# Routing weights as two fp32r parts in blocks of 32 rows, one bias product per half batch, and nineteen more identity products

## The reference, cut to what matters

```python
logits = xf @ Wg + bg
probs = jax.nn.softmax(logits, axis=-1)
w, idx = jax.lax.top_k(probs, TOP_K)
w = w / jnp.sum(w, axis=-1, keepdims=True)
comb = jnp.sum(jax.nn.one_hot(idx, E, dtype=xf.dtype) * w[..., None], axis=1)
h = jax.nn.relu(jnp.einsum('nd,edh->enh', xf, W1) + b1[:, None, :])
y = jnp.einsum('enh,ehd->end', h, W2) + b2[:, None, :]
out = jnp.einsum('end,ne->nd', y, comb)
```

## Time and profile before

| | |
|---|---|
| runs before, us | 179.95, 180.94, 181.54; median 180.94 |
| profiled execution, us | 182.35 |
| its span, first to last instruction, us | 180.5 |
| PE busy in the span | 163.2 us, 712 instructions |
| DVE, ACT, POOL busy | 118.7, 102.9, 73.0 us |
| mean granted TensorE clock | 0.981 |
| DMA | 7.23 MB, mean 40 GB/s |

### The profile page before, as it was taken

One profiled execution on the slowest core, in us unless ns is written; L12 is line 12 of the kernel. 1 busy time (PEld: TensorE's weight loads), 2 busy tenths in 40 slices (PEclk: granted clock), 3 DMA queues, 4 the chain that ended last, 5 costly groups with the idle time before them and its releaser, 6 DMA issues.

```text
span 180.5 us, 2419 instructions
## 1 busy us (share of the span) xinstructions
PE 163.2 (90%) x712; PEld 96.3 (53%) x712; DVE 118.7 (66%) x380; ACT 102.9 (57%) x185; POOL 73.0 (40%) x120
## 2 busy tenths in 40 slices
PE   1999998979885799999999999999999899999992
PEld 1554655434332348555655644367667566677781
DVE  3758898984367488866568557666769664566541
ACT  3446638846753324899747577673664446645621
POOL 2399272262372043976621041352522244322500
PEclk9999999999999966999999999999999999999999
DMA  6798600000000234300000000000000000001001
GB/s 177 264 315 178 210 8 0 2 0 2 2 0 0 57 75 101 77 0 0 0 4 0 0 0 0 4 0 2 0 5 0 0 0 0 0 0 58 4 0 58
DMA packets 5570, 7.23 MB, mean 40 GB/s; under 512 B 749, under 2 KB 3606, under 8 KB 5558
## 3 DMA queue, kind: packets, MB, share of 16 engines
q1 hardware_dynamic: 5142, 6.66, 13.0%
q10 hardware_dynamic: 416, 0.42, 0.7%
HBM read 5.17 MB, written 0.52 MB: 32 GB/s over the span
## 4 chain that ended last, share of the span: by engine, by line
PE 65%; DVE 18%; ACT 8%; issue 4%; POOL 2%; DMA 1%; SPq 0%; DVEq 0%; POOLq 0%; ACTq 0%
PE bank L1120 7%; PE bank L1156 6%; PE bank L1268 5%; PE bank L1175 4%; PE bank L1270 4%; PE bank L1269 4%; PE bank L1251 3%; PE bank L1253 3%; PE bank L1252 3%; PE bank L1178 3%; DVE stats L1325 3%; PE bank L1237 3%; PE bank L914 2%; PE bank L1196 2%; POOL rstd L526 2%
## 5 line engine op out<-in xcount | busy, mean ns | idle before, releaser
L644 POOL TENSOR_TENSOR pair<-early,pair 128x512 fp32r<-128x512 f32 x16 | 20.5, 1287 | 38.6 <-ACT pair L861 38.6
L1600 DVE SCALAR_TENSOR_TENSOR pair<-bank,pair 128x512 fp32r<-128x512 f32 x32 | 21.6, 690 | 19.0 <-ACT pair L868 18.9
L1512 DVE TENSOR_REDUCE nmax<-bank 128x2 f32<-128x308 f32 x64 | 26.3, 471 | 11.4 <-PE bank L1120 11.2
L836 ACT ACTIVATE prob<-bank 128x512 f32<-128x512 f32 x40 | 22.7, 597 | 6.4 <-PE bank L1156 6.1
L1120 PE MATMUL bank<-pair,q_s 97*128 97x308 f32 x64 | 22.1, 411 | 0.7 <-ACT q_s L813 0.3
L868 ACT ACTIVATE pair<-bank 128x512 fp32r<-128x512 f32 x32 | 18.8, 596 | 6.1 <-PE bank L1253 4.8
L861 ACT ACTIVATE pair<-early 128x512 fp32r<-128x512 f32 x16 | 10.1, 632 | 21.1 <-DVE early L1596 21.1
L526 POOL TENSOR_TENSOR rstd<-vare,m_half 128x4 f32<-128x4 f32 x10 | 10.4, 1044 | 24.4 <-DVE vare L1330 21.1
L1120 PEld LDWEIGHTS bank<-pair,q_s 97*128 97x128 f32 x64 | 13.2, 214 | 12.0 <-DVE nmax L1512 7.1
L1156 PE MATMUL bank<-q_s,pair 112*128 112x512 f32 x40 | 17.5, 452 | 0.1
L1268 PE MATMUL bank<-pair,w_h 128*128 128x512 f32 x32 | 14.1, 440 | 0.0
(11 more groups left out here) (239 smaller groups left out, 314.0 us busy)
## 6 DMA issues: line engine op xcount, KB each, us to landing
w_s<-in_w SPq DMA_DIRECT2D x1, 1024.0 KB, 7.3
prob<-in_w SPq DMA_DIRECT2D x1, 1024.0 KB, 12.8
q_s<-q_late SPq DMA_DIRECT2D x12, 64.0 KB, 2.0
q_s<-pair SPq DMA_DIRECT2D x9, 64.0 KB, 2.0
x_t<-in_x SPq DMA_DIRECT2D x2, 256.0 KB, 3.1
wf_s<-in_w_ffn SPq DMA_DIRECT2D x1, 512.0 KB, 4.8
row<-in_rows SPq DMA_DIRECT2D x1, 260.0 KB, 3.9
wc_s<-in_w_ctx ACTq DMA_DIRECT2D x1, 256.0 KB, 4.1
```

The lines of the kernel that those rows point to most:

```text
L644: pool.tensor_tensor(ec_l[:, n % NEC], ec[:, n % NEC], ec_h[:, n % NEC].bitcast(F32), ALU.subtract).then_inc(ec_lo, 1)
L836: nc.scalar.activation(prob[:, u % NPR], bank[ST[u % 3]][:], ACT.Exp).then_inc(prob_ready, 1)
L1512: dve.tensor_reduce(nmax[:, b, q, j, g:g + 2], item_bank("score", n)[:, 0:2 * TK].rearrange("p (h k) -> p h k", k=TK), AX.X, ALU.max, nega ...
L1600: dve.scalar_tensor_tensor(out=hid_l[:, g % NH], in0=bank[RING[g % 4]][:], scalar=0.0, in1=hid_h[:, g % NH].bitcast(F32), op0=ALU.max, op1 ...
```

## The change: what it does

The routing weights are split into two fp32r parts instead of three bf16 ones. The parts lie in four blocks of 32 rows of which eight are used (high, low, high, low), so that the turned weights have 104 rows (3 x 32 + 8). The first two blocks feed the spreads. b2 lies in four blocks of the same kind (high, high, low, low), and one 104-row product replaces three of 24 rows. `pick_e` moves into the memory of `sel`, `comb_f` into that of `q_late`; ACT therefore waits for the last moves out of `q_late` before its first copy. b2 is loaded four times instead of three. `comb_part` is now one buffer for both batch entries, cleared once at the start by DVE, and entry 1 waits for the turn of entry 0.

The identity products grow from 35 to 54: 4, 3, 1, 1 and 2 in the first stage, one more after the second cell step, 5 ahead of `turn_in(1)` and 2 in `query(0)`.

```diff
+PART = 32
+ROWS_B2 = 3 * PART + E
...
-        b2_part = sb("b2_part", [3 * E, 3, P], BF16)
-        pick_e = sb("pick_e", [3 * E, E, P], BF16)
-        hot = sb("hot", [3 * E, E])
+        b2_h = sb("b2_h", [ROWS_B2, P], F32R)
+        b2_part = sb("b2_part", [ROWS_B2, P], F32R)
+        hot = sb("hot", [ROWS_B2, E])
...
-            for p in range(3):
-                sp.dma_start(b2_s[p * E:(p + 1) * E], b2).then_inc(ld_b2, 16)
+            for p in range(4):
+                sp.dma_start(b2_s[p * PART:p * PART + E], b2).then_inc(ld_b2, 16)
...
-                    link(pool.tensor_copy(b2_part[:, 0], b2_s[:]))
-                    link(pool.tensor_tensor(b2_r[:], b2_s[:], b2_part[:, 0], ALU.subtract))
-                    link(pool.tensor_copy(b2_part[:, 1], b2_r[:]))
-                    pool.tensor_tensor(b2_part[:, 2], b2_r[:], b2_part[:, 1], ALU.subtract).then_inc(b2_ready, 1)
+                    link(pool.memset(b2_part[:].bitcast(F32), 0.0))
+                    block_of = [slice(p * PART, p * PART + E) for p in range(4)]
+                    for rows_p, to in zip(block_of, (b2_part, b2_part, b2_h, b2_h)):
+                        link(pool.tensor_copy(to[rows_p], b2_s[rows_p]))
+                    for rows_p in block_of[2:]:
+                        pool.tensor_tensor(b2_part[rows_p], b2_s[rows_p], b2_h[rows_p].bitcast(F32), ALU.subtract)\
+                            .then_inc(b2_ready, 1)
...
+                    if b == 0:
+                        for moved in q_moved[HQ - 1:]:
+                            act.wait_ge(moved, 48)
+                    copy_out(bank[TB[0]][0:ROWS_B2], comb_f[:, b], comb_tr, b + 1,
...
+            pe.wait_ge(consts_ready, 3)
+            keep_busy(4, 7)
             key_value_bias(0)
+            keep_busy(3, 7)
...
             keys_values(0)
+            keep_busy(1, 7)
             turn_a(0)
             key_value_bias(1)
+            keep_busy(1, 7)
             queries(0)
             keys_values(1)
+            keep_busy(2, 7)
             state(0)
...
             pe.wait_ge(gates_act, 6)
-            keep_busy(7, 0)
+            keep_busy(8, 0)
...
             def turn_in(b):
+                if b == 1:
+                    keep_busy(5, 0)
...
                 b, q = divmod(m, HQ)
+                if m == 0:
+                    keep_busy(2, 0)
                 pe.wait_ge(q_lo, b + 1)
...
-                        last = pe.transpose(comb_ps[:, j * P:(j + 1) * P], comb_part[:, b, j], ident_b[:])
+                        rows_j = comb_part[:, j].bitcast(F32).rearrange("p k e -> p (k e)")[:, 0:ROWS_B2]
+                        last = pe.transpose(first[0:ROWS_B2, j * P:(j + 1) * P], rows_j, ident[:])
...
-                    for k in range(3):
-                        pe.matmul(y, b2_part[:, k], comb_f[:, b], start=k == 0, stop=False)
+                    pe.matmul(y, b2_part[:], comb_f[:, b], start=True, stop=False)
...
+                    if b:
+                        dve.wait_ge(comb_tr, b)
+                    link(dve.tensor_copy(comb_part[:, :, 0:4:2, 0:E], twice(comb[:, b])))
+                    dve.tensor_tensor(comb_part[:, :, 1:4:2, 0:E], twice(comb[:, b]),
+                                      comb_part[:, :, 0:4:2, 0:E].bitcast(F32), ALU.subtract).then_inc(comb_ready, 1)
```

More of the change, by code:

```diff
@@ L210, in two_blocks @@
         sel = sb("sel", [P, HQ, SEL_W], F32R)
+        pick_e = sel[0:ROWS_B2].rearrange("p q w -> p (q w)")[:, 0:E * P].rearrange("p (e o) -> p e o", o=P)
         k_hl = q_late[:, :, 0:NB * TKP]
@@ L241, in two_blocks @@
         comb = sb("comb", [P, NB, NJ, E])
-        comb_r = sb("comb_r", [P, NB, NJ, E])
-        comb_part = sb("comb_part", [P, NB, NJ, 3, E], BF16)
-        comb_f = k0[0:3 * E].rearrange("p c d -> p (c d)").bitcast(BF16).rearrange("p (b t) -> p b t", b=NB)
+        comb_part = sb("comb_part", [P, NJ, 4, PART], F32R)
+        comb_f = q_late[0:ROWS_B2]
         y_f = q_m
@@ L557, in _ @@
                     .then_inc(sel_ready, 1)
-            link(pool.tensor_tensor(hot[:], ident[0:3 * E, 0:E], ident[0:3 * E, E:2 * E], ALU.add))
-            pool.tensor_tensor(hot[:], hot[:], ident[0:3 * E, 2 * E:3 * E], ALU.add).then_inc(hot_ready, 1)
+            pool.tensor_tensor(hot[:], ident[0:ROWS_B2, 0:E], ident[0:ROWS_B2, PART:PART + E], ALU.add)\
+                .then_inc(hot_ready, 1)
             pool.wait_ge(hot_ready, 1)
@@ L632, in _ @@
                 if m == 4:
[L633 to L638 removed]
+                    pool.wait_ge(ld_b2, 64)
+                    link(pool.memset(b2_part[:].bitcast(F32), 0.0))
[5 more added lines that the diff above has]
+                            .then_inc(b2_ready, 1)
+                    pool.wait_ge(b2_ready, 2)
                 if m in (1, 5):
@@ L796, in pick_copies @@
                 act.wait_ge(hot_ready, 1)
-                nc.scalar.activation(pick_e[:], hot[:].rearrange("p (e o) -> p e o", o=1).broadcast_to([3 * E, E, P]),
+                nc.scalar.activation(pick_e, hot[:].rearrange("p (e o) -> p e o", o=1).broadcast_to([ROWS_B2, E, P]),
                                      ACT.Copy).then_inc(pick_ready, 1)
@@ L1236, in comb_spread @@
                     wait_item(LAST[XP[0][1]])
-                pe.matmul(bank[spread_bank(n)][:], pick_e[:, e], comb_f[:, b], start=True, stop=True)\
+                pe.matmul(bank[spread_bank(n)][:], pick_e[:, e], comb_f[0:ROWS_B2, b], start=True, stop=True)\
                   .then_inc(comb_b_mm, 1)
@@ L1258, in down @@
                 if e == 0 and c == 0:
[L1260 removed]
+                    pe.wait_ge(b2_ready, 2)
                     if b == 0:
                         pe.wait_ge(o_ev_ready, NB * HQ)
[L1263 to L1264 removed]
+                    pe.matmul(y, b2_part[:], comb_f[:, b], start=True, stop=False)
                 g = n * HC + c
@@ L1351, in _ @@
             link(dve.memset(nm_part[:], 0.0))
+            link(dve.memset(comb_part[:].bitcast(F32), 0.0))
             dve.memset(nm_part[:, :, :, :, 0:1], 1.0)
@@ L1581, in tail, with twice @@
                     link(dve.tensor_tensor(comb[:, b], hit1w[:, b], hit2w[:, b], ALU.add))
-                    link(dve.tensor_copy(comb_part[:, b, :, 0], comb[:, b]))
-                    link(dve.tensor_tensor(comb_r[:, b], comb[:, b], comb_part[:, b, :, 0], ALU.subtract))
-                    link(dve.tensor_copy(comb_part[:, b, :, 1], comb_r[:, b]))
-                    dve.tensor_tensor(comb_part[:, b, :, 2], comb_r[:, b], comb_part[:, b, :, 1],
-                                      ALU.subtract).then_inc(comb_ready, 1)
+                    def twice(ap):
+                        return ap.rearrange("p j (o e) -> p j o e", o=1).broadcast_to([P, NJ, 2, E])
+                    if b:
[3 more added lines that the diff above has]
+                                      comb_part[:, :, 0:4:2, 0:E].bitcast(F32), ALU.subtract).then_inc(comb_ready, 1)
             def scaled(n):
```

5 lines of the change are left out of this document (1 added, 4 removed).

## The result

The changed kernel takes 178.3 us (median of 6 runs, 177.59 to 179.93) against 181.24 us of the kernel before beside it (6 runs, 179.75 to 183.96). The ratio is 0.9881, 95% interval 0.9834 to 0.9929: faster by 1.2%, where 2.6% were forecast. The time lies inside the range; the case that came is the rival *Experts only*, not the likeliest.

A forecast was written before the change was run, and what follows sets the result against it. PE was taken to bound the kernel (65% of the chain of waits). Gains of 3.9 + 1.0 + 0.6 = 5.5 us took 182.35 to 176.9, and 0.7 us for the lower median gave 176.2 us; range 174.4 to 179.2.

The forecast's parts named there:

- Experts only: Rival, chance 0.26: expert gains come, the clock at 65 us still falls, first stage even or 1 us late; 177.0 to 178.5.
- Terms 1 to 3: Expert stage: spreads without gaps 2.6 us, fewer bias products 1.4, splitting and turning weights 0.2, less 0.3 for ACT/DVE: 3.9 gained.
- The gap stays: Rival, chance 0.13: switching row count or operand, not bf16, breaks the load stream; spreads gain nothing; 178.3 or 179.9 us.
- Term 3: Splitting and turning the routing weights: DVE drops two dependent operations, the f32 turn is longer; gain 0.2 us.
- The hand-over: First three spreads, in the attention: each is waited for anyway, so no gain or loss, 0 us.
- Term 5: First stage: identity products raise PE's clock sooner, partly under the DMA wait; gain 0.6 us.
- case of a rise by 9.5 us: First stage: if the clock rises by then, the added 1.9 us is about won back; gain 0.2 us.
- Term 4: Start of the second attention: eight new products in PE's idle time keep the clock up; gain 1.0 us.
- The baseline: Profiled 182.35 us against median 180.94: half of the 1.4 us difference, 0.7 us, taken off the forecast time.

The follow-up runs named there:

- routing alone: The changed kernel without its nineteen new identity products; median 176.69 us, ratio 0.9777 to before; further sets 177.59 us (0.9791) and 178.55 us (0.9884).
- the repeat of the change: The changed kernel, unaltered, run again beside two variants on the same chip; median 178.82 us, ratio 0.9861 to the kernel before.
- identity products alone: The kernel before with the nineteen new identity products and nothing else; median 181.44 us, ratio 1.0028.
- the repeat of before: The kernel before, unaltered, run again to see the granted clock of each execution; median 182.6 us, ratio 1.0005.
- extra product: The changed kernel with one more fp32r product, here of 24 rows, ahead of each of the 16 spreads; 185.66 us (one execution).

## Why the prediction was off

**Terms 1 to 3, the experts (-3.9): right in size, wrong in reason.** The stage gave 3.57 us in the profile: starts 0.23 us apart, rounds of 3.03 us, the bias from L1271 at 121.33 to L1286 at 122.27, 0.94 us, as forecast. But the 0.27 us that a spread lost was put down to the turn between fp32r and bf16; it is the price of a product of 64 rows or fewer among full ones. The forecast came out because the new spread has 104 rows, and rows 10, on which it leaned, had 97 and 112. So the size came right with the reason wrong, which is luck. The rival *The gap stays* named the row count, but gave it the wrong consequence: the change switches to a row count that costs nothing. The Trainium skill (TensorEngine Tiling (Array Packing), Overview and Tiling Modes) lists modes of 64 and of 32 rows beside the full array of 128, and says "Changing tiling mode (not just tile) drains the TensorE". The edge between 64 and 80 rows and the equal price of 24 and 64 agree with it; that it is a change of mode, or a drain, no run here shows. The prediction weighed instead what the Trainium skill says of fast loading (TensorE: Matmul & The Clock Gate, Weight-path perf modes) and gave it no weight in the sum. That was right: the load of 0.19 us hides, except at the hand-over. Term 3 had a wait of under 0.6 us before the first spread of entry 1; it is 0.67 us, where it was 0.72.

**The hand-over, costed at 0: +0.4 us.** "The first three spreads stand in the attention, each waited for anyway" holds for the wait as it was; but it is PE that waits here, and its wait grew. Timeline, PE, of the change:
```profile
112.06 0.60 PE L1242 MATMUL bank<-ident,comb_part 128*104 128x128 f32 x4
...
113.42 0.49 PE L1255 MATMUL bank<-q_late,sel 104*128 104x512 f32 x1 [0.53 <-ACT q_late L674]
```
The turn takes 0.60 us where it took 0.39, ACT's copy is waited for 0.53 us where it was 0.26, and an unhidden load of 0.19 stands where 0.09 stood. So of 3.57 us some 3.2 reach the end, and the shortest executions agree: 179.61 before, 176.46 with routing alone, 3.15 us.

**Term 5, the first stage (-0.6): this step failed.** It gave +0.51 us in the profile and +1.1 us between shortest executions (177.59 against 176.46; 180.73 against 179.61). The working had the cost about right: 1.9 us in the open if the clock does not rise sooner. Its case of a rise by 9.5 us even came, in the repeat of the change (timeline, PE):
```profile
10.69 1.10 PE L965 MATMUL bank<-a_f,w_s 128*128 128x512 f32 x2
```
ACT had the queries at 11.83 there, 0.15 us ahead of rows 3, where 0.2 were worked out. The failure was to book this as a return of the products. The upper level came by 9.5 us in some executions with no product ahead (routing alone) and at 13 or later in others; with eleven it came by 9.3 us in the repeat, by 11.4 in the first profile, and after 14 in another (identity products alone: L928 at 13.47 takes 1.06 us where 0.59 is the upper level's). One profiled execution of before, with a late rise, was taken for what every execution does. Over all profiled executions, ACT gets the first queries at 11.81 to 13.71 us in the eight with eleven products, and at 10.62 to 12.05 in the ten without the seven that stand in the open: 1.1 us later at an early rise and 1.7 at a late one. The chain of waits of the change, 3 to 14 us, shows where it lies, L1031 (start, us, what):
```profile
3.90 2.00 PE bank L932 x2
5.90 1.39 PE bank L1031 x3
7.29 0.85 PE bank L936 x2
```

**Term 4, the low clock at 65 us (-1.0): right for the profile, not for the runs.** The two profiled executions differ there by 1.25 us. But before has the low stretch in part of its executions only, and the change has it too. In the mean the late products give 0.4 us or nothing, within what the runs can tell; what they did come with is that the longest stretches are missing.

**The baseline.** The profiled execution of before (182.35 us) was longer than nearly three of four of its executions (59 of 80). Half of its distance to the median was credited as clock that could not be won back. The late products gave 0.4 us at most, so nothing in the runs supports keeping the other half.

By the shortest executions routing gives -3.2 us and the first-stage products +1.1; with -0.4 to 0 for the late ones that is -2.1 to -2.5 us. The ratio of 0.9881 is 2.1 us; the medians of all executions lie 2.9 us apart in the first set and 2.7 beside the repeat (181.49 and 178.82). By the means of all executions the same steps are -3.4, +0.9 and -0.4 us, each uncertain by about 0.4, together -2.9. So of the 5.5 us that the terms add up to, term 5 accounts for the largest miss, some 1.5 us, before term 4 and the hand-over. Routing alone has the shortest executions; its three sets have ratios of 0.9777, 0.9791 and 0.9884. In the median it does not stand clear of the versions with late products and none in the open (0.9804 to 0.9809).

## What to carry to other kernels

A product whose contraction (the rows that are summed over) has 64 rows or fewer, put singly into a stream of full ones, costs more than its length: look for starts 0.3 us apart where 0.23 is the pace, and fill the operand with zero rows to 80 or more before changing types or dropping products. Products that are only to keep the clock up belong under a wait that is there anyway, and even there their return has to be seen over many executions: the mean granted clock of each, beside its time. Where executions of one kernel lie several per cent apart, compare the shortest and the shares of long ones, and do not credit a change with a disturbance that one profiled execution happened to have.

## What the runs showed of the hardware

- Start distances at full clock are 0.23 us for 512 columns in fp32r, with 80, 104, 112 and 128 rows, and single bf16 products of 104 and 128 rows among them fit the same pace (0.69 us for three distances). Between bf16 products it is 0.22 us (the five identity products at 57.21 in the change). With 24 and 64 rows in fp32r the way in, through and out again takes 0.37 us more, with 24 rows in bf16 0.27 us more.
- Few columns of weights cost something too: the first value product, 128 rows by 32 columns, starts 0.33 us after the full one ahead of it (73.78 to 74.11, above).
- A weight load of fp32r with 104 or 128 rows takes 0.19 us and is hidden under the product before; one of 24 rows takes 0.18 us and starts only with its own product (PEld, 24 rows, extra product):
```profile
159.12 0.18 PEld L1255 LDWEIGHTS bank<-q_late,sel 24*128 24x128 f32 x1 [0.36 <-issue]
```
- The granted clock of one program falls at other places from execution to execution: at 0.50 from 65 to 70 us, at some 59 to 62 us in the repeat of before, from 60 to 72 us in one profiled execution of routing alone and not at all in the other two. After an unbroken run from 2.0 us on, PE left its lower level at about 9.2 us in one execution, at 11 us in another, and after 14 us in a third.
